# An attention kernel with an MLP woven into it: the first MLP product and its Gelus in two blocks of four, and the second product four slots later

## The chip, the cores and the metric

The kernel runs on one core of a Trainium2 chip. The metric is the device time of one execution in microseconds (us), lower being better. Five engines work side by side, each through its own list of instructions in order: TensorE (PE, with PEld for its weight loads), VectorE (DVE), ScalarE (ACT), GpSimd (POOL) and SyncE (SP), which starts most DMA transfers. They wait for each other through semaphores.

## The reference, cut to what matters

The input is eight images of 256 channels x 1024 positions in float32. Each image goes through two stages: an attention over its 1024 positions with 8 heads, and then, on the tokens, a linear attention and an MLP on a downsampled band. The parts that matter here:

```python
# stage 1, per image: softmax attention over 1024 positions, 8 heads
qkv = einsum('oc,bcl->bol', w_qkv, group_norm(x)) + b_qkv
weight = softmax(einsum('bct,bcs->bts', q * scale, k * scale))
x = x + (w_proj @ einsum('bts,bcs->bct', weight, v) + b_proj)
# stage 2, per image: linear attention, then the MLP on the low band
t = t + linear_attention(layer_norm(t))
ll, lh, hl, hh = haar(layer_norm(t))
h = gelu(einsum('bfc,hc->bfh', interp(ll), fc1_w) + fc1_b)     # 1024 hidden
ll_new = einsum('bfh,oh->bfo', h, fc2_w) + fc2_b               # back to 128
t = t + inverse_haar(ll_new, lh, hl, hh)
```

## The kernel before, in words

**Slots.** Stage 1 of an image is cut into 64 units, one for each of the 8 heads and each block of 128 keys. A unit is a 128x1024 tile of scores. TensorE makes it (`scores`, line 636), VectorE takes the row maxima (`maximum`, line 1025), ScalarE takes the exponential and its sums (`exponentials`, line 887), and every four units TensorE multiplies the result with the values (`weigh_values`, line 651, into `ps_o`), after VectorE has inverted the sums (line 1031) and GpSimd has scaled the values with them (line 1297). There are two score buffers, `ps_s0` and `ps_s1`: the scores of unit s+2 wait for the exponential of unit s. A unit's number within its image is called its slot here.

**What fills the slots.** Everything else is put into the slots by tables, one for each engine and kind of image (`PE_STEADY`, `ACT_STEADY`, `DVE_STEADY` and so on). An entry such as `"fc2": (51, 53, 55, 56)` says after which unit each piece of a step is put into that engine's list. Within a slot the pieces stand in the order of the table's keys. While image i is in stage 1, stage 2 of image i-1 and the first steps of image i+1 run in its slots. The first image has no stage 2 beside it. Images 1 to 6 use the steady tables, the last image uses `PE_LAST` and its like, which lack the steps for a next image, and stage 2 of the last image runs alone in an epilogue (`PE_TAIL` and so on). The order is fixed when the program is built: an engine whose next instruction waits does nothing else.

In TensorE's list slot s begins with the scores of unit s+1. In the lists of ScalarE and VectorE it begins with the exponential or the maximum of unit s. So an exponential "50" is the one that opens slot 50 on ScalarE.

**The work banks.** All pieces but the scores and `ps_o` share two banks, `work0` and `work1`, in turn (`banks`). A piece waits until the one before it in its bank has been read (`claim`, `READ`). The second MLP product adds four pieces into one bank (fc2 0 to 3, entries 1 to 3 in `LATER_STEPS`), so from fc2 0 to fc2 3 all other pieces go to the other bank.

**The MLP.** `ll` (line 777) makes the low band, ScalarE copies it to `band` (line 968). `fc1` n, of eight (line 782), multiplies `band` with 128 columns of the first weights, and ScalarE puts the Gelu of it into `hid` (line 971; the profile calls it `shared`). `fc2` (line 787) waits for all eight Gelus, VectorE adds the bias and subtracts the old band (line 1184), SyncE spreads the rows (line 543), and VectorE adds them to the output in slots 1 and 5 of the next image (`late_up`, line 1191). `pk0`, the first two key projections for the next image (line 663), lies among them in slots 52 and 53: ScalarE reads it as the high part (line 928), then VectorE as the low part (line 1070). `rT` are transposes (line 698) that ScalarE copies out (line 975).

Of the kernel before, what the change touches and what calls it, by code (L numbers as in the profile page):

```python
# [42 lines left out]
for _name, _width in (("bq", 2), ("bk", 2), ("bproj", 2), ("bqk", 4), ("lepe_w", 6), ("lepe_bias", 6),  # L43
# [37 lines left out]
    "values": (2, 6, 10, 14, 18, 22, 26, 30, 34, 38, 42, 46, 50, 54, 58, 62),  # L81
}
ACT_STEADY = {
    "copy": (3, 4, 34, 35), "x1T": (9, 10, 11, 14), "lnT": (15, 15, 16, 16),
    "qk": (18, 18, 21, 22, 24, 25, 28, 30), "den": (32,), "rT": (47, 50, 50, 51), "ll": (48,),
    "fc1": (49, 49, 49, 49, 49, 49, 49, 49), "pq1": (11, 13), "pk1": (20, 20), "apply": (41, 41), "pq0": (43, 44),
    "pk0": (52, 53),
}
DVE_STEADY = {
# [5 lines left out]
}  # L95
# [6 lines left out]
PE_LAST = {  # L102
    "proj": (4, 5, 7, 8), "x1T": (9, 9, 10, 13), "lnT": (15, 15, 16, 16), "qk": (17, 18, 21, 22, 24, 25, 28, 29),
    "kT": (23, 26, 30, 31), "kv": (28, 33), "den": (31,), "denT": (32,), "out": (35, 37, 41, 42),
    "uT": (39, 40, 43, 43), "rT": (48, 48, 50, 51), "ll": (48,), "fc1": (48, 48, 49, 49, 49, 49, 49, 49),
    "fc2": (53, 54, 56, 57), "pq1": (11, 12), "pv1": (0, 0), "pk1": (19, 19),
    "values": (2, 6, 10, 14, 18, 22, 26, 30, 34, 39, 43, 46, 50, 55, 58, 63),
}
ACT_LAST = {
    "copy": (3, 4, 36, 39), "den": (31,), "x1T": (9, 10, 11, 14), "lnT": (15, 15, 16, 16),  # L110
    "qk": (18, 18, 21, 22, 24, 25, 28, 30), "rT": (47, 48, 51, 53), "ll": (48,),
    "fc1": (49, 49, 49, 49, 49, 49, 49, 49), "pq1": (11, 13), "pk1": (19, 20),
}
DVE_LAST = {
# [5 lines left out]
}  # L120
POOL_LAST = {
# [1374 lines left out]
```

How the kernel before makes its waits and increments, by code:

```python
        def load_image(eng, b):  # L440
            eng.wait_ge(made["pk1"], 2 * b)
            eng.dma_start(xg[:, :, :], x_v[b]).then_inc(x_in, DMA)
# [1 line left out]
        def stack_q(eng, b, g):  # L445
            eng.wait_ge(lo_done, 8 * b + 4 * g + 2)
            for h in range(HG):
                for row, part in enumerate((hi, hi, lo, lo)):
                    eng.dma_start(q_st[g][D * row:D * row + D, h, :].bitcast(F32),
                                 part[D * h:D * h + D, :].bitcast(F32)).then_inc(q_stacked, DMA)
# [1 line left out]
        def stack_k(eng, b, g, half, done_units=None):  # L453
            hi_k, lo_k = key_parts(b, g)
            if half == 0:
                eng.wait_ge(lo_done, 8 * b + 4 * g + 4)
            elif done_units is not None:
                eng.wait_ge(scores_ready, done_units)
            else:
                eng.wait_ge(lo_done, 4)
            cols = slice(half * HALF, half * HALF + HALF)
            signal = k_stacked_b if half else k_stacked_a
            for h in range(HG):
                for row, part in enumerate((hi_k, lo_k, hi_k, lo_k)):
                    eng.dma_start(k_st[D * row:D * row + D, h, cols].bitcast(F32),
                                 part[D * h:D * h + D, cols].bitcast(F32)).then_inc(signal, DMA)
# [1 line left out]
        def stack_first_k(eng, pieces, signals):  # L471
            eng.wait_ge(lo_done, 1 + nth_split(0, ("pk0", 0)))
            for h, row in pieces:
                part = (hi_first, lo_first, hi_first, lo_first)[row]
```

## Time and profile before

| | |
|---|---|
| median of three runs | 1381.69 us (1381.51 to 1382.86) |
| profiled execution, its own time | 1382.15 us |
| its span | 1380.4 us |
| PE / DVE / ACT / POOL busy | 88% / 72% / 64% / 34% |
| mean granted TensorE clock | 0.975 |

The span runs from the first instruction to the last; the profiled execution's own time is 1.75 us longer. Busy shares are over the whole span. In the timeline a row is one instruction, or several alike (x4), with its start, its duration, and behind it in brackets how long the engine had been idle and who released it. A row of a table of stretches has the stretch (from the span's start), its length, the busy time of PE, PEld, DVE, ACT and POOL with the instructions in brackets, the granted TensorE clock as a share of full speed, the busy share of the DMA engines and their GB/s. A matmul of float32 operands shows as two records, so one `fc1` piece is x2 and one `fc2` piece is x4.

### The profile page before, as it was taken

Reading aid. Unit: us, or ns where it says so; the run is one execution under the profiler, and the core shown is the slowest. Engines: PE = TensorE matmul, PEld = TensorE weight load, DVE = VectorE, ACT = ScalarE, POOL = GpSimd, SP = SyncE. Lnnn points to the kernel's source line nnn. Section 1 sums busy time; section 2 is a strip of 40 time slices with the busy share of each in tenths; the row PEclk is TensorE's granted clock in tenths of the full one; section 3 lists DMA queues with packets and bytes.
Section 4 is the critical chain, followed back from the end, with each engine's and each line's share of the span. In section 5 each row is a group of like instructions: output and inputs, shape, how many; then the busy total and the mean of one; then the engine's idle time right before and its main releaser. Section 6 shows DMA issues by size and latency. Waiting matters only on the chain.

```text
span 1380.4 us, 21964 instructions
## 1 busy us (share of the span) xinstructions
PE 1211.1 (88%) x7868; PEld 629.9 (46%) x7868; DVE 991.3 (72%) x1607; ACT 881.9 (64%) x1457; POOL 465.6 (34%) x623
## 2 busy tenths in 40 slices
PE   6888899899988999899988999899998999878846
PEld 5544544545444454444445454444444444433433
DVE  2676688848887597857889487866889487874551
ACT  1667677576766667576776768676776767656402
POOL 2001017510384015720195014730176103830450
PEclk8999999999999999999999999999999999999977
DMA  8243324133433225233252224332341333300101
GB/s 267 54 119 73 91 63 108 48 70 97 109 76 92 54 67 132 57 75 103 67 120 71 53 81 124 60 92 71 89 112 53 69 90 84 81 31 16 46 17 46
DMA packets 51355, 111.28 MB, mean 81 GB/s; under 512 B 15504, under 2 KB 15760, under 8 KB 50992
## 3 DMA queue, kind: packets, MB, share of 16 engines
q1 hardware_dynamic: 48576, 100.85, 30.0%
q0 software_dynamic: 2480, 8.78, 2.0%
q8 instruction: 63, 1.03, 0.3%
q14 instruction: 44, 0.36, 0.1%
q10 hardware_dynamic: 192, 0.26, 0.1%
HBM read 21.75 MB, written 8.39 MB: 22 GB/s over the span
## 4 chain that ended last, share of the span: by engine, by line
PE 44%; DVE 29%; POOL 8%; ACT 8%; issue 6%; SPq 3%; DMA 2%; DVEq 0%; POOLq 0%; ACTq 0%
DVE negmax L1025 15%; PE ps_s L636 10%; PE ps_o L651 7%; ACT probs L887 6%; PE work L663 4%; PE work L710 4%; POOL x L1356 4%; PE work L724 4%; PE work L782 4%; DVE ln_st L1090 3%; DVE tok L1101 3%; PE work L787 3%; POOL csum L1353 1%; DVE t L1177 1%; DVE lo L1070 1%
## 5 line engine op out<-in xcount | busy, mean ns | idle before, releaser
L887 ACT ACTIVATE probs<-ps_s,negmax 128x1024 f32<-128x1024 f32 x512 | 569.7, 1113 | 322.2 <-DVE negmax L1025 314.9
L1025 DVE TENSOR_REDUCE negmax<-ps_s 128x1 f32<-128x1024 f32 x512 | 620.0, 1215 | 192.1 <-PE ps_s L636 189.6
L636 PE MATMUL ps_s<-q_st,k_st 128*128 128x512 f32 x1024 | 404.6, 478 | 59.4 <-ACT probs L887 49.3
L636 PEld LDWEIGHTS ps_s<-q_st,k_st 128*128 128x128 f32 x1024 | 164.8, 191 | 285.5 <-ACT probs L887 167.0
L651 PE MATMUL ps_o<-probs,v_scaled 128*32 128x512 f32 x2048 | 248.8, 603 | 2.8 <-POOL v_scaled L1297 2.8
L1297 POOL TENSOR_TENSOR v_scaled<-v_tok,rsums 128x128 f32<-128x128 f32 x128 | 51.2, 400 | 545.0 <-DVE rsums L1031 544.2
L663 PE MATMUL work<-xg,w_qkv 128*128 128x512 f32 x256 | 119.6, 592 | 0.0
L724 PE MATMUL work<-ln_ch,w_qk 128*128 128x512 f32 x236 | 113.8, 604 | 2.1 <-DVE k_ch L1203 2.1
L651 PEld LDWEIGHTS ps_o<-probs,v_scaled 128*32 128x32 f32 x2048 | 53.7, 109 | 127.0 <-issue 119.8
L1356 POOL TENSOR_TENSOR x<-x,csum 128x1024 f32<-128x1024 f32 x45 | 106.8, 2373 | 2.0
L887 ACT ACTIVATION_READ_ACCUMULATOR probs<-ps_s,negmax 128x1 f32 x512 | 99.1, 194 | 0.0
L782 PE MATMUL work<-band,w 128*128 128x512 f32 x116 | 59.2, 645 | 9.1 <-ACT band L968 6.1
L663 PEld LDWEIGHTS work<-xg,w_qkv 128*128 128x128 f32 x256 | 48.2, 189 | 40.9 <-issue 33.4
L675 PEld LDWEIGHTS work<-w_qkv,xg 128*128 128x128 f32 x512 | 63.2, 196 | 4.0 <-DVE lo L1070 1.4
L675 PE MATMUL work<-w_qkv,xg 128*128 128x128 f32 x512 | 63.6, 279 | 0.0
L724 PEld LDWEIGHTS work<-ln_ch,w_qk 128*128 128x128 f32 x236 | 42.6, 190 | 41.6 <-issue 29.3
L1328 POOL TENSOR_TENSOR ln_var<-ln_mv,con 128x2 f32<-128x2 f32 x64 | 13.6, 212 | 129.0 <-DVE ln_mv L1095 129.0
L710 PE MATMUL work<-att,w_proj 128*128 128x512 f32 x120 | 56.8, 597 | 0.0
L787 PE MATMUL work<-shared,w 128*128 128x512 f32 x112 | 53.2, 597 | 1.4 <-ACT ln_ch L975 1.4
L1353 POOL TENSOR_SCALAR csum<-ln_ch,par 128x1024 f32<-128x1024 f32 x45 | 53.8, 1195 | 0.0
L971 ACT ACTIVATE shared<-work,par 128x512 f32<-128x512 f32 x58 | 39.3, 686 | 14.9 <-PE work L782 14.8
L1331 POOL TENSOR_TENSOR ln_rs<-ln_var,con 128x2 f32<-128x2 f32 x64 | 44.7, 699 | 5.0
(150 smaller groups left out, 1418.5 us busy)
## 6 DMA issues: line engine op xcount, KB each, us to landing
q_st<-hi SPq DMA_DIRECT2D x128, 128.0 KB, 2.4
q_st<-lo SPq DMA_DIRECT2D x120, 128.0 KB, 2.4
k_st<-t SPq DMA_DIRECT2D x224, 64.0 KB, 2.0
k_st<-hi SPq DMA_DIRECT2D x128, 64.0 KB, 2.0
k_st<-lo SPq DMA_DIRECT2D x128, 64.0 KB, 2.0
x<-in_x SPq DMA_DIRECT2D x8, 1024.0 KB, 4.8
out_x<-ln_ch SPq DMA_DIRECT2D x16, 512.0 KB, 2.7
xg<-in_x POOLq DMA_DIRECT2D x7, 1024.0 KB, 5.7
```

Of the source, the lines that this page charges most:

```text
L636: mm = pe.matmul(ps_s[s % 2][:, half * HALF:half * HALF + HALF], k_st[:, h, j * P:j * P + P], q_st[g][:, h, half * HALF:half * HALF + HALF ...
L651: mm = pe.matmul(ps_o[D * h:D * h + D, cols], v_scaled[:, j % 2, D * h:D * h + D], probs[:, j % 2, h, cols], start=(j == 0), stop=(j == NB ...
L663: mm = pe.matmul(bank(tile)[:, :], w_qkv[:, c, col:col + P], xg[:, c, half * HALF:half * HALF + HALF], start=(c == 0), stop=(c == NC - 1))
L675: mm = pe.matmul(bank(tile)[:, P * n:P * n + P], xg[:, c, P * nb:P * nb + P], w_qkv[:, c, col:col + P], start=(c == 0), stop=(c == NC - 1))
L710: mm = pe.matmul(ps[:, :], w_proj[:, g, P * c:P * c + P], att[:, g, half * HALF:half * HALF + HALF], start=(g == 0), stop=(g == 1))
L724: mm = pe.matmul(ps[:, :], w_qk[:, c, col:col + P], ln_ch[:, c, 1 + half * HALF:1 + half * HALF + HALF], start=(c == 0), stop=(c == NC - 1))
L782: pe.matmul(ps[:, :], w1[:, P * n:P * n + P], band[:, :], start=True, stop=True)\
L787: mm = pe.matmul(ps[:, :], w2[:, k, :], hid[:, k, :], start=(k == 0), stop=(k == 7))
L887: act.activation(probs[:, j % 2, h, :], ps_s[s % 2][:, :], ACT.Exp, bias=negmax[:, s % 4:s % 4 + 1], accum_out=sums[:, j % 2, h:h + 1]).th ...
L1025: dve.tensor_reduce(negmax[:, s % 4:s % 4 + 1], ps_s[s % 2][:, :], AX_X, ALU.max, negate=True)\
L1353: pool.tensor_scalar(lepe_product, ln_ch[:, c, tap:tap + L], param("lepe_w", 3 * c + tap), param("lepe_bias", 3 * c + tap), ALU.mult, ALU. ...
L1356: pool.tensor_tensor(x1[:, c, :], x1[:, c, :], lepe_product, ALU.add).then_inc(lepe_step, 1)
```

## The change

Only the tables of the steady images and of the last one are changed. On TensorE, fc1 4 to 7 go from slot 49 to slots 54 and 55, and fc2 from slots 51, 53, 55, 56 (last image 53, 54, 56, 57) to slots 56 to 59. On ScalarE, Gelus 4 to 7 go from slot 49 to slot 55. On VectorE the step that reads fc2 goes from slot 57 (last image 58) to slot 60. The epilogue's tables stay.

```diff
 PE_STEADY = {
-    "fc1": (48, 48, 49, 49, 49, 49, 49, 49), "fc2": (51, 53, 55, 56), "pq1": (11, 12), "pv1": (0, 1),
+    "fc1": (48, 48, 49, 49, 54, 54, 55, 55), "fc2": (56, 57, 58, 59), "pq1": (11, 12), "pv1": (0, 1),
...
 ACT_STEADY = {
-    "fc1": (49, 49, 49, 49, 49, 49, 49, 49), "pq1": (11, 13), "pk1": (20, 20), "apply": (41, 41), "pq0": (43, 44),
+    "fc1": (49, 49, 49, 49, 55, 55, 55, 55), "pq1": (11, 13), "pk1": (20, 20), "apply": (41, 41), "pq0": (43, 44),
```

ScalarE's list in a steady image, before, from the exponential that opens slot 49 on (`probs` are exponentials, `shared` Gelus, `ln_ch` copies of `rT`, `t` high parts of `pk0`):

```order
 L887 ACTIVATE probs,sums<-ps_s,negmax 128x1024
 L971 ACT_TABLE_LOAD
 L971 ACTIVATE shared<-work,par 128x512 x8
 L887 ACT_TABLE_LOAD
 L887 ACTIVATE probs,sums<-ps_s,negmax 128x1024
 L975 COPY ln_ch<-work 128x512 x2
 L887 ACTIVATE probs,sums<-ps_s,negmax 128x1024
 L975 COPY ln_ch<-work 128x512
 L887 ACTIVATE probs,sums<-ps_s,negmax 128x1024
 L928 ACTIVATE t<-work,par 128x512
 L887 ACTIVATE probs,sums<-ps_s,negmax 128x1024
 L928 ACTIVATE t<-work,par 128x512
```

The same place now, from the exponential that opens slot 53 on:

```order
 L887 ACTIVATE probs,sums<-ps_s,negmax 128x1024
 L928 ACTIVATE t<-work,par 128x512
 L887 ACTIVATE probs,sums<-ps_s,negmax 128x1024 x2
 L971 ACT_TABLE_LOAD
 L971 ACTIVATE shared<-work,par 128x512 x4
 L887 ACT_TABLE_LOAD
 L887 ACTIVATE probs,sums<-ps_s,negmax 128x1024 x12
```

In slot 49 four Gelus are left between a pair of table loads, and four others stand with a second pair of table loads behind the exponential of slot 55.

TensorE's list in a steady image, before, from the pieces of slot 51 on (`work<-con,t` is rT 2 and 3, `work<-shared` fc2, `work<-xg` pk0, `ps_s` scores):

```order
 L698 MATMUL work0<-con,t2 128x128 x4
 L787 MATMUL work1<-shared,w2 128x512 x2
 L636 MATMUL ps_s1<-q_st1,k_st 128x512 x2
 L663 MATMUL work0<-xg,w_qkv 128x512 x2
 L636 MATMUL ps_s0<-q_st1,k_st 128x512 x2
 L787 MATMUL work1<-shared,w2 128x512 x2
 L663 MATMUL work0<-xg,w_qkv 128x512 x2
 L636 MATMUL ps_s1<-q_st1,k_st 128x512 x2
 L651 MATMUL ps_o<-probs,v_scaled 32x512 x8
 L636 MATMUL ps_s0<-q_st1,k_st 128x512 x2
 L787 MATMUL work1<-shared,w2 128x512 x2
```

TensorE's list now, from the second `pk0` piece in slot 53 on (`work<-band` is fc1):

```order
 L663 MATMUL work0<-xg,w_qkv 128x512 x2
 L636 MATMUL ps_s1<-q_st1,k_st 128x512 x2
 L782 MATMUL work1<-band,w1 128x512
 L782 MATMUL work0<-band,w1 128x512
 L651 MATMUL ps_o<-probs,v_scaled 32x512 x8
 L636 MATMUL ps_s0<-q_st1,k_st 128x512 x2
 L782 MATMUL work1<-band,w1 128x512
 L782 MATMUL work0<-band,w1 128x512
 L636 MATMUL ps_s1<-q_st1,k_st 128x512 x2
 L787 MATMUL work1<-shared,w2 128x512 x2
 L636 MATMUL ps_s0<-q_st1,k_st 128x512 x2
 L787 MATMUL work1<-shared,w2 128x512 x2
```

The two `pk0` pieces, which shared `work0` while fc2 held `work1`, now lie in different banks; fc1 4 and 5 stand in front of the values product of slot 54, and the fc2 pieces follow one another in neighbouring slots.

## Rows read from the trace of the kernel before

**Rows 1.** The page, busy time and share of each engine.

```profile
PE 1211.1 (88%) x7868; PEld 629.9 (46%) x7868; DVE 991.3 (72%) x1607; ACT 881.9 (64%) x1457; POOL 465.6 (34%) x623
```

**Rows 2.** Groups on ScalarE: table loads, busy us and mean ns of one.

```profile
L971 ACT ACT_TABLE_LOAD x8 | 10.3, 1283 | 0.1
L887 ACT ACT_TABLE_LOAD x7 | 9.0, 1283 | 0.1
```

**Rows 3.** Stretches of image 4: between exponentials 49, 50, 56 and 61.

```profile
759.75:770.86 11.11, 10.26 (x36) 4.22 (x40) 2.45 (x2) 9.18 (x14) 0.00 (x0) 1.00 0.32 70
770.86:786.35 15.49, 14.71 (x63) 6.97 (x55) 7.59 (x9) 9.82 (x18) 0.40 (x1) 1.00 0.06 13
786.35:795.59 9.24, 8.54 (x47) 4.55 (x45) 6.66 (x7) 5.94 (x10) 0.80 (x2) 1.00 0.43 104
```

**Rows 4.** Timeline of image 4 from exponential 49 to Gelu 3.

```profile
759.75 1.13 ACT L887 ACTIVATE probs<-ps_s,negmax 128x1024 f32<-128x1024 f32 x1
760.99 1.28 ACT L971 ACT_TABLE_LOAD   x1
762.28 1.26 ACT L971 ACTIVATE shared<-work,par 128x512 f32<-128x512 f32 x2
...
765.05 0.69 ACT L971 ACTIVATE shared<-work,par 128x512 f32<-128x512 f32 x1 [0.17 <-PE work L782]
```

**Rows 5.** Timeline of image 4, slots 51 to 55.

```profile
773.79 1.12 ACT L887 ACTIVATE probs<-ps_s,negmax 128x1024 f32<-128x1024 f32 x1
...
775.38 1.03 PE L636 MATMUL ps_s<-q_st,k_st 128*128 128x512 f32 x2
...
776.24 1.88 PE L663 MATMUL work<-xg,w_qkv 128*128 128x512 f32 x4
776.42 1.11 ACT L887 ACTIVATE probs<-ps_s,negmax 128x1024 f32<-128x1024 f32 x1 [0.94 <-DVE negmax L1025]
777.68 0.90 PE L636 MATMUL ps_s<-q_st,k_st 128*128 128x512 f32 x2
...
780.13 1.88 PE L663 MATMUL work<-xg,w_qkv 128*128 128x512 f32 x4
...
782.70 1.11 ACT L887 ACTIVATE probs<-ps_s,negmax 128x1024 f32<-128x1024 f32 x1
782.83 0.75 DVE L1070 SCALAR_TENSOR_TENSOR t<-work,par,t 128x512 fp32r<-128x512 f32 x1 [2.01 <-ACT t L928]
```

**Rows 6.** Timeline of image 4, slots 55 to 58.

```profile
784.26 0.73 PE L636 MATMUL ps_s<-q_st,k_st 128*128 128x512 f32 x2
...
784.81 1.11 ACT L887 ACTIVATE probs<-ps_s,negmax 128x1024 f32<-128x1024 f32 x1 [0.92 <-DVE negmax L1025]
784.83 1.88 PE L787 MATMUL work<-shared,w 128*128 128x512 f32 x4
785.03 1.22 DVE L1025 TENSOR_REDUCE negmax<-ps_s 128x1 f32<-128x1024 f32 x1 [0.32 <-PE ps_s L636]
...
787.01 1.88 PE L787 MATMUL work<-shared,w 128*128 128x512 f32 x4
...
788.33 1.02 PE L636 MATMUL ps_s<-q_st,k_st 128*128 128x512 f32 x2
...
790.45 1.92 PE L651 MATMUL ps_o<-probs,v_scaled 128*32 128x512 f32 x16
```

**Rows 7.** Timeline of SyncE in image 4, the spreading of the band.

```profile
793.88 2.51 SPq L543 DMA_DIRECT2D csum<-band  x4
```

**Rows 8.** Timeline of VectorE, `late_up` in slot 1 of the next image.

```profile
802.41 1.22 DVE L1191 SCALAR_TENSOR_TENSOR ln_ch<-csum,ln_ch 128x1024 f32<-128x1024 f32 x1
```

**Rows 9.** Stretch of image 3 between exponentials 49 and 50.

```profile
600.55:612.38 11.83, 11.58 (x36) 4.93 (x40) 2.45 (x2) 9.28 (x13) 0.00 (x0) 0.86 0.28 63
```

**Rows 10.** Stretches of the last image between exponentials 50, 56 and 61.

```profile
1248.07:1259.69 11.62, 9.56 (x47) 4.21 (x40) 6.09 (x6) 8.06 (x15) 0.40 (x1) 1.00 0.00 0
1259.69:1269.64 9.95, 8.20 (x34) 3.44 (x34) 6.86 (x8) 5.94 (x10) 0.40 (x1) 1.00 0.24 53
```

More of the change, by code:

```diff
@@ L104 @@
     "kT": (23, 26, 30, 31), "kv": (28, 33), "den": (31,), "denT": (32,), "out": (35, 37, 41, 42),
-    "uT": (39, 40, 43, 43), "rT": (48, 48, 50, 51), "ll": (48,), "fc1": (48, 48, 49, 49, 49, 49, 49, 49),
-    "fc2": (53, 54, 56, 57), "pq1": (11, 12), "pv1": (0, 0), "pk1": (19, 19),
+    "uT": (39, 40, 43, 43), "rT": (48, 48, 50, 51), "ll": (48,), "fc1": (48, 48, 49, 49, 54, 54, 55, 55),
+    "fc2": (56, 57, 58, 59), "pq1": (11, 12), "pv1": (0, 0), "pk1": (19, 19),
     "values": (2, 6, 10, 14, 18, 22, 26, 30, 34, 39, 43, 46, 50, 55, 58, 63),
@@ L111 @@
     "qk": (18, 18, 21, 22, 24, 25, 28, 30), "rT": (47, 48, 51, 53), "ll": (48,),
-    "fc1": (49, 49, 49, 49, 49, 49, 49, 49), "pq1": (11, 13), "pk1": (19, 20),
+    "fc1": (49, 49, 49, 49, 55, 55, 55, 55), "pq1": (11, 13), "pk1": (19, 20),
 }
```

4 rows, old and new, of tables (DVE_LAST, DVE_STEADY) are left out of this document.

## The prediction, written before the changed kernel ran

> **What bounds the kernel now.** I read the page first. TensorE is busy for 88% of the span and ScalarE for 64% [rows 1], so on average TensorE comes first and ScalarE has room. The change touches one stretch of each image, though, so I went to the groups on ScalarE next. There the table loads are to be seen: 8 in front of Gelus and 7 back to exponentials, 1283 ns each [rows 2]; the eighth Gelu block is the epilogue's. Each image pays the way out and back once.
>
> Then I cut image 4 into stretches at the exponentials. The slot of the Gelus takes 11.11 us, the next six slots 15.49 us and five more 9.24 us. TensorE is busy for 10.26, 14.71 and 8.54 us of these [rows 3], so over the 35.84 us it has only 2.33 us of gaps that show, and 0.70 of these lie in the last five slots. Two things bound the stretch by turns: the Gelu block, where exponentials wait behind ScalarE's list, and TensorE's own list in slots 50 to 57.
>
> At last I read the timeline. In the Gelu block ScalarE sets the pace: exponential 49 starts at 759.75, the table load at 760.99 and Gelus 0 and 1 at 762.28. Gelu 3 starts at 765.05, behind a wait, since fc1 2 and 3 can only be made once Gelus 0 and 1 have freed their banks [rows 4]. Outside the block I take four delays from the rows. From the start of an exponential to the scores that wait for it it is 1.26 us (776.42 to 777.68). From scores to the next piece on TensorE it is 0.86 us where TensorE had not been waiting (775.38 to 776.24) [rows 5], and 0.57 us where it had (784.26 to 784.83). From scores to their maximum it is 0.77 us and the maximum takes 1.22. A `pk0` or fc2 piece takes 1.88 us to its end and 1.32 us to the next piece (787.01 to 788.33) [rows 6].
>
> **The change part by part, steady image.** I write it down in image 4's times, all from exponential 50 on to be read 3.80 us earlier.
>
> Block A, slot 49. Four Gelus stay, with both loads. From exponential 49 to the start of Gelu 3 it is 5.30 us; 0.69 of Gelu, 1.28 of load and 0.04 of steps between them bring exponential 50 at 7.31 in place of 11.11 us [rows 3, 4]. Gain: 3.80 us.
>
> Slots 50 to 55. fc2 0 and 1 are gone from here, and `pk0` 1 no longer waits for the bank of `pk0` 0. Exponential 50 to 52 stay: ScalarE waits there for rT copies and for a maximum that VectorE does only after inverting sums. Scores 53 start 0.32 us earlier, at 775.06, where exponential 51 (773.79) lets them go; `pk0` 0 then starts at 775.63 and ends at 777.5, and its high part is read in front of exponential 53, at 778.2. Scores 54 wait for exponential 52 and stay at 777.68. Now `pk0` 1 follows them directly, at 778.25 in place of 780.13, ScalarE can read its high part at 780.2, and exponential 54 starts at 780.8 in place of 782.70 [rows 5]. Exponential 55 keeps its distance of 2.1 us (782.70 to 784.81 [rows 6]), since the low part (0.75) and the maximum (1.22) stand between: 782.85. Gain: 1.95 us.
>
> Block B, slot 55. It adds two loads and four Gelus behind exponential 55. fc1 4 is made before, at 780.5, and fc1 5 after the low part of `pk0` 1 has been read, at 781.65; both are ready when the load ends. TensorE does the values product and scores 56 in the meantime (to 785.4), so it loses little by fc1 6 waiting for Gelu 4. The block has block A's shape: 7.31 us to exponential 56 (790.15) where it was 1.54. Cost: 5.77 us. As exponential 56 stood at 786.35, the three parts together give -3.80 - 1.95 + 5.77 = 0.0 us there. I bound block B by 6.5 us (loads and Gelus alone: 1.24 + 2 x 1.30 + 4 x 0.66) and 8.5 us (TensorE late by 1.2 us, its extra wait for the low part), and take 7.31, the nearest row.
>
> The Trainium skill speaks against such a split: "ScalarE: Activation LUTs", in "Rules for kernel authors", says to group functions by table set and finish one set before switching. The same page, in "What ACT_TABLE_LOAD costs", puts a switch at about 2.66 us, a load of 1283 ns and a drain as long again. This trace agrees with the load only: Gelu 0 starts 1.29 us after the load does, and the load 1.24 us after exponential 49 [rows 4]. By the page 14 more switches would cost some 37 us of ScalarE's time, by the rows 18 us; my sum uses neither, but block B as timed.
>
> Slots 56 to 60. Here lie all four fc2 pieces now, of which two came before exponential 56 until now and a third just before. fc2 0 waits for Gelu 7 and runs at 788.9, under the load back to exponentials, at no cost. Exponential 57 follows exponential 56 by 1.20 us (791.35), its maximum being ready. Scores 58 wait for exponential 56: 791.41; exponential 58 comes at 793.45. fc2 1 stands at 791.98, so scores 59 come at 793.3 and exponential 59 at 795.65. fc2 2 (794.2) and the values product (795.5, 1.92 long [rows 6]) stand in front of scores 60, at 797.4: exponential 60 at 799.5. fc2 3 (798.0) makes scores 61 start at 799.3, and in front of maximum 61 VectorE now waits for fc2 3 (799.9) and does the band's step (0.75): exponential 61 at 801.95, where it was 795.59. From exponential 56 on that is 11.80 us in place of 9.24 [rows 3]. Cost: 2.56 us. Bounds: 1.2 us, if half of it is covered by the gaps, and 3.44 + 0.75 = 4.2 us, if two fc2 pieces of 1.72 and the step lie bare. After slot 61 units go at their round trip from exponential to scores to maximum to exponential, through which a delay passes whole: `pv0` 1 and slot 63 keep their distances.
>
> The move of VectorE's step delays SyncE's list as well: the spreading of the band, now at 793.88 and 2.51 us long [rows 7], starts some 7 us later (800.7). Behind it are queued the late keys, not wanted before slot 16, and waiting for it is `late_up` in slot 1, at 802.41 [rows 8], now 808.8. From the last issue to `late_up` it was 6.0 us (796.4 to 802.4) and is 5.6 us now (803.2 to 808.8). Cost: none; without this cover each microsecond of lateness would stand in every image.
>
> Per steady image: 0.0 + 2.56 = 2.56 us, six times: 15.4 us.
>
> Last image. It has no `pk0`. Block A gives 3.80. Taking fc2 0 out of slot 53 brings exponential 55 about 0.9 us earlier. The slot of block B grows from 2.75 us to 7.3, so the six slots take 11.62 - 0.9 + 4.55 = 15.3 us; the next five take 12.5 in place of 9.95 [rows 10]. That is -3.80 + 3.65 + 2.55 = 2.4 us. I take 2.3. First image and epilogue are unchanged.
>
> **Sum:** 1382.15 of the profiled execution + 15.4 + 2.3 = 1399.85 us. The median of the runs shown is 0.46 below that execution, so I predict 1399.4 us. A change under 0.2% (2.8 us) counts as none.
>
> **Rivals.** (1) Faster: fc2 hides in the gaps. TensorE stands at 88%, and behind block B two score tiles wait ready, so units could run at their round trip, which is 1.26 + 0.77 + 1.22 + 0.1 = 3.35 us for two slots: exponential 57 after 1.20 and four more at 1.68 make 7.9 us, 1.3 less than before. Seven images: 9.2 us, 1372.5. It decides whether TensorE has room for 3.44 us of fc2 where 0.70 us of gaps showed [rows 3]; for it speaks that ScalarE idles a third of the time, against it that a slot with fc2 takes 0.86 + 1.32 = 2.18 us already. (2) No change: the delay of slots 56 to 61 is caught up in slots 61 to 63, so only the 0.0 us at exponential 56 remains: about 1382. Against it: a round trip bounds those slots. (3) Slower still: the clock. TensorE now idles about 1.3 us in front of scores 53, 0.7 before scores 54 and 0.6 before scores 58. In image 3 the granted clock was 0.86 of full speed on average in the slot of the Gelus, a piece of it at 1.2 GHz, and that slot took 11.83 us in place of 11.11 [rows 3, 9]. If each of seven images pays such 0.7 us once or twice more, it is 5 to 10 us on top: about 1407.
>
> **How the numbers follow.** Forecast 0.72, its own range 1391 to 1408 (1.2 us up or down per image, by the bounds above); rival 3 0.14; rival 1 0.07; rival 2 0.05; a switch that stops ScalarE for twice its load, 0.02, at 1417, by another 1.28 for each of 14 loads (this is where the page's drain would lead; against it stands Gelu 0's start, [rows 4]). Range 1389 to 1410, which leaves out rivals 1 and 2 and the upper end of 3. Faster 0.07, the same 0.05, slower 0.88.
>
> **What would show it.** Table loads: 15 in front of Gelus and 14 back, at 1283 ns. Between exponentials 49 and 50: 7.3 us. Between 50 and 56: 19.3. Between 56 and 61: 11.8, with fc2 between scores in each slot. `pk0` 1 some 1.9 us after the scores 54 no more. I am wrong if slots 56 to 61 take under 9.3 us, if block B takes under 6 us, or if the band's landing holds `late_up`.

## The result, and the profile after

The changed kernel takes 1404.56 us (median of four runs, 1402.84 to 1407.14) against 1381.92 us before: the ratio is 1.0164, with a 95% interval of 1.0144 to 1.0184. A second set of four runs on another occasion gave 1403.17 us, a ratio of 1.0144 (1.0120 to 1.0168) to the kernel before as it ran there, 1383.14 us. Slower, then, and within the range; the forecast of +17.7 us was 5 us short of the median. The profiled execution took 1402.84 us with a span of 1401.0 us, 20.6 us more than the span of before. What follows is about these 20.6 us.

On the page TensorE's and ScalarE's shares stay almost where they were [rows 1]:

```profile
PE 1216.1 (87%) x7868; PEld 631.1 (45%) x7868; DVE 992.8 (71%) x1607; ACT 898.6 (64%) x1471; POOL 465.5 (33%) x623
```

ScalarE is busy for 16.7 us more, with 14 instructions more. The 14 are table loads, 7 in front of Gelus and 7 back, each as long as before [rows 2]:

```profile
L971 ACT ACT_TABLE_LOAD x15 | 19.2, 1283 | 0.3
L887 ACT ACT_TABLE_LOAD x14 | 18.0, 1283 | 0.2
```

The stretches of image 4 answer to [rows 3], cut at exponentials 49, 50, 55, 56 and 61 (length, busy time of PE, PEld, DVE, ACT and POOL, granted clock, DMA share, GB/s):

```profile
767.96:775.25 7.29, 6.44 (x28) 3.03 (x32) 2.45 (x2) 6.42 (x9) 0.00 (x0) 1.00 0.49 106
775.25:787.32 12.07, 9.72 (x40) 4.51 (x36) 6.18 (x7) 8.59 (x16) 0.40 (x1) 1.00 0.01 2
787.32:794.60 7.28, 6.09 (x27) 2.33 (x26) 2.53 (x3) 6.41 (x9) 0.40 (x1) 1.00 0.44 106
794.60:806.73 12.13, 11.66 (x55) 5.93 (x53) 5.64 (x6) 5.91 (x11) 0.40 (x1) 1.00 0.10 24
```

| image 4, us | before | foretold | after |
|---|---|---|---|
| exponential 49 to 50 | 11.11 | 7.31 | 7.29 |
| 50 to 55 | 13.95 | 12.00 | 12.07 |
| 55 to 56 (block B) | 1.54 | 7.31 | 7.28 |
| 56 to 61 | 9.24 | 11.80 | 12.13 |
| together | 35.84 | 38.42 | 38.77 |

Exponential 56 stands 26.64 us after exponential 49 where it stood 26.60 us after it: the first three terms cancel, as foretold, and the loss comes to light behind it. The same figures repeat within 0.02 us in all six steady images, but for slot 49 of image 6, 8.11 us long.

Block B is a copy of block A. Its timeline:

```profile
787.32 1.11 ACT L887 ACTIVATE probs<-ps_s,negmax 128x1024 f32<-128x1024 f32 x1 [0.92 <-DVE negmax L1025]
788.54 1.28 ACT L971 ACT_TABLE_LOAD   x1
789.83 1.26 ACT L971 ACTIVATE shared<-work,par 128x512 f32<-128x512 f32 x2
790.57 1.98 PE L782 MATMUL work<-band,w 128*128 128x512 f32 x4 [0.78 <-ACT shared L971]
...
792.60 0.69 ACT L971 ACTIVATE shared<-work,par 128x512 f32<-128x512 f32 x1 [0.17 <-PE work L782]
...
793.30 1.28 ACT L887 ACT_TABLE_LOAD   x1
793.43 1.95 PE L787 MATMUL work<-shared,w 128*128 128x512 f32 x4 [0.41 <-ACT shared L971]
794.60 1.11 ACT L887 ACTIVATE probs<-ps_s,negmax 128x1024 f32<-128x1024 f32 x1
```

TensorE waits for ScalarE twice in it: 0.78 us in front of fc1 6 and 0.41 us in front of fc2 0. fc2 0 does run under the second load. Slots 51 to 54, answering to [rows 5]:

```profile
779.45 0.73 PE L636 MATMUL ps_s<-q_st,k_st 128*128 128x512 f32 x2 [1.34 <-ACT probs L887]
...
782.08 0.73 PE L636 MATMUL ps_s<-q_st,k_st 128*128 128x512 f32 x2 [0.18 <-ACT probs L887]
...
782.65 1.88 PE L663 MATMUL work<-xg,w_qkv 128*128 128x512 f32 x4
...
786.15 1.12 PE L782 MATMUL work<-band,w 128*128 128x512 f32 x2 [0.30 <-DVE t L1070]
```

`pk0` 1 follows scores 54 by 0.57 us (782.08 to 782.65), where it came 2.45 us after them (777.68 to 780.13 [rows 5]). TensorE idles for 1.34 us in front of scores 53, since nothing stands there any more to fill the wait. fc1 5 waits for the low part of `pk0` 1, as foretold. Slots 57 to 61, answering to [rows 6]:

```profile
798.60 1.88 PE L787 MATMUL work<-shared,w 128*128 128x512 f32 x4
...
800.41 1.92 PE L651 MATMUL ps_o<-probs,v_scaled 128*32 128x512 f32 x16
802.26 0.73 PE L636 MATMUL ps_s<-q_st,k_st 128*128 128x512 f32 x2
802.83 1.88 PE L787 MATMUL work<-shared,w 128*128 128x512 f32 x4
803.03 1.23 DVE L1025 TENSOR_REDUCE negmax<-ps_s 128x1 f32<-128x1024 f32 x1 [3.01 <-PE ps_s L636]
...
804.75 0.75 DVE L1184 SCALAR_TENSOR_TENSOR band<-work,par,band 128x512 f32<-128x512 f32 x1 [0.41 <-PE work L787]
```

Maximum 60 waits 3.01 us for its scores, behind fc2 2 and the values product, and VectorE waits again, 0.41 us, for fc2 3. From the fc2 piece to the values product it is 1.81 us, not the 1.32 us that separates such a piece from scores.

The band still comes in time. SyncE spreads it from 805.53 on and `late_up` runs at 813.54, 5.6 us after the last issue (it was 6.0 [rows 7, 8]):

```profile
805.53 2.42 SPq L543 DMA_DIRECT2D csum<-band  x4
```

```profile
813.54 1.22 DVE L1191 SCALAR_TENSOR_TENSOR ln_ch<-csum,ln_ch 128x1024 f32<-128x1024 f32 x1
```

The last image, answering to [rows 10]. Its slot 49 took 11.10 us before:

```profile
1236.97:1248.07 11.10, 10.25 (x36) 4.22 (x40) 2.45 (x2) 9.17 (x14) 0.00 (x0) 1.00 0.01 1
```

After, cut at exponentials 49, 50, 56 and 61:

```profile
1253.71:1261.83 8.12, 7.87 (x28) 3.69 (x32) 2.45 (x2) 6.53 (x10) 0.00 (x0) 0.79 0.00 0
1261.83:1277.34 15.51, 11.88 (x47) 4.90 (x40) 6.09 (x6) 13.27 (x21) 0.40 (x1) 0.89 0.00 1
1277.34:1290.13 12.79, 11.97 (x44) 5.21 (x43) 6.96 (x9) 6.02 (x10) 0.40 (x1) 1.00 0.00 1
```

It takes 36.42 us where it took 32.67: +3.75 us. The first row is 0.8 us longer than block A elsewhere, at a granted clock of 0.79, which means part of it at 1.2 GHz. The second row holds another fall of the clock, to 0.89 on average. Before, the clock was full in all of these slots.

Added up between exponentials 49 and 61: six images at +2.93 us are 17.6, less 0.7 because the clock fell in the Gelu block of two of them before and of one after, and +3.75 for the last image: 20.6 us. The other stretches differ by up to 2 us each way (the start of the program +1.9, slots 29 to 43 of the six images -1.2 together) and cancel.

### The profile page after: what moved, and what is told of

It is laid out like the page before. It is cut to its first block, busy times and chain, and to the rows that moved or that the text cites. A ratio compares the mean times of both kernels' runs of the same rounds, so it can differ in the third digit from the quotient of the medians.

```text
span 1401.0 us, 21978 instructions
## 1 busy us (share of the span) xinstructions
PE 1216.1 (87%) x7868; PEld 631.1 (45%) x7868; DVE 992.8 (71%) x1607; ACT 898.6 (64%) x1471; POOL 465.5 (33%) x623
## 4 chain that ended last, share of the span: by engine, by line
PE 40%; DVE 30%; ACT 11%; POOL 7%; issue 7%; SPq 4%; DMA 2%; DVEq 0%; POOLq 0%; ACTq 0%
DVE negmax L1025 15%; PE ps_s L636 9%; ACT probs L887 7%; PE ps_o L651 7%; PE work L710 4%; PE work L724 4%; PE work L663 3%; DVE ln_st L1090 3%; POOL x L1356 3%; DVE tok L1101 3%; PE work L787 3%; PE work L782 3%; SPq L468 1%; DVE lo L1070 1%; DVE t L1177 1%
## 5 line engine op out<-in xcount | busy, mean ns | idle before, releaser
L782 PE MATMUL work<-band,w 128*128 128x512 f32 x116 | 62.5, 656 | 16.4 <-ACT shared L971 8.8
```

What stands on the lines that cost most here:

```text
L782: pe.matmul(ps[:, :], w1[:, P * n:P * n + P], band[:, :], start=True, stop=True)\
```

## The experiments

Two theories stood at first. Theory A was the prediction's: TensorE's list sets the pace here, the split cancels against slots 49 to 55, and the late fc2 pieces are the cost. Theory B was that the cost is the 14 table loads, 14 x 1.28 = 18 us, which happens to give the same total.

### One block of Gelus, fc2 late (e1)

```diff
-    "fc2": (51, 53, 55, 56)    # PE, steady; last image (53, 54, 56, 57)
+    "fc2": (56, 57, 58, 59)
-    "fc2": (57,)               # DVE, steady; last image (58,)
+    "fc2": (60,)
```

> The kernel before, with one block of eight Gelus in slot 49 as it was, and only fc2 moved to slots 56 to 59 (VectorE's step to slot 60). Two table loads per image as before. Theory A (the cost comes from the fc2 pieces packed into slots 56 to 59, while the split itself is paid back by slots 50 to 55): slot 49 stays at 11.1 us, exponentials 50 to 55 take 12.0 in place of 13.95 us, exponentials 55 to 61 about 14.0 in place of 10.8 us, together +1.3 us in each of seven images: 1391 us. Theory B (the cost is the 14 added table loads, 18 us in all, and the place of fc2 costs nothing): the same as before, 1382 us, or less, down to 1369 if the 1.95 us of slots 52 to 54 stay gained.

Measured: 1397.42 us, ratio 1.0107 (1.0082 to 1.0132). Image 4, exponentials 49, 50, 56, 61:

```profile
763.80:774.90 11.10, 10.25 (x36) 4.21 (x40) 2.45 (x2) 9.17 (x13) 0.00 (x0) 1.00 0.33 71
774.90:788.52 13.62, 10.49 (x51) 4.72 (x44) 7.49 (x9) 9.80 (x18) 0.40 (x1) 1.00 0.06 15
788.52:801.28 12.76, 12.76 (x59) 6.77 (x58) 6.86 (x7) 6.02 (x11) 0.80 (x2) 1.00 0.28 69
```

The gain of 1.9 us in the middle row and the loss of 3.5 us in the last are there without any added load: +1.64 us per steady image, which I had put at 1.3. The last image loses 4.8 us (37.46 for 32.67), but part of that is the clock: its slot 55 ran wholly at 1.2 GHz and took 4.93 us.

```profile
1267.52:1272.45 4.93, 4.87 (x19) 1.24 (x19) 1.23 (x1) 1.21 (x4) 0.00 (x0) 0.50 0.00 0
```

Theory B alone is out, since it allowed 1382 us at most. Theory A had the direction but not the size: it had said 1391 us. But the changed kernel has 1.29 us more per image than this one, so the split was not free.

### One block of eight in slot 55 (e2)

```diff
-    "fc1": (48, 48, 49, 49, 49, 49, 49, 49), "fc2": (51, 53, 55, 56)   # PE
+    "fc1": (54, 54, 55, 55, 55, 55, 55, 55), "fc2": (56, 57, 58, 59)
-    "fc1": (49, 49, 49, 49, 49, 49, 49, 49)                            # ACT
+    "fc1": (55, 55, 55, 55, 55, 55, 55, 55)
```

> fc2 as in the changed kernel (56 to 59), all eight fc1 pieces and Gelus in one block in slots 54 and 55, so two table loads per image. Theory A: slot 49 falls from 11.1 to about 2 us, 52 and 53 give 1.95 us, slot 55 takes 11.1 in place of 1.54 us, slots 56 to 60 cost 2.6 us as in the changed kernel: +1.1 us per image, about 1390 us. Theory B: no added loads, so 1382 us, the time of before.

Measured: 1406.77 us, ratio 1.0174 (1.0147 to 1.0200). Both theories missed, at 1390 and 1382 us. Image 5, exponentials 50, 55 and 56:

```profile
934.04:947.29 13.25, 11.44 (x53) 5.27 (x55) 7.40 (x8) 8.59 (x16) 0.40 (x1) 1.00 0.15 32
947.29:958.38 11.09, 9.91 (x35) 3.52 (x34) 2.53 (x3) 9.16 (x13) 0.40 (x1) 1.00 0.40 95
```

Slot 49 fell to 1.78 us and slot 55 grew to 11.09, as expected, but slot 50 grew from 2.94 to 4.13 us, so slots 50 to 54 gained 0.7 and not 1.95 us, and in two images they took 15 us at a lower clock. A Gelu block gives something back: while ScalarE is held, TensorE makes the next scores, a first pair of transposes and the values product of slot 50. Without the block, slot 50 has this product to do itself, and ScalarE waits 1.97 us there for the transposes behind it. The stretch from 49 to 61 takes 38.25 us, +2.4, with no load added.

### Relu for Gelu in both kernels (e3, e4)

```diff
-    act.activation(hid[:, n, :], ps[:, :], ACT.Gelu, bias=param("b1", n)).then_inc(gelu_done, 1)
+    act.activation(hid[:, n, :], ps[:, :], ACT.Relu, bias=param("b1", n)).then_inc(gelu_done, 1)
```

The kernel before:

> The kernel before with a Relu in place of each Gelu, which takes all table loads but the first out of the program (the MLP's function is thereby another). Theory A: the first load of a block was half hidden behind fc1 0 and 1, the second behind the values product: 2 us less per image, about 1367 us. Theory B: loads stand bare, 2.57 us less in each of eight images: 1361 us.

The changed kernel:

> The changed kernel with a Relu in place of each Gelu (again another function in the MLP, no table loads but the first). To be set against the kernel before with Relu. Theory A: the two differ by 2 us or so in each image (fc2 in slots 56 to 59 costs the same, and fc2 0 has no load to hide under any more), so this runs at about 1380 us, 13 us over the other. Theory B: without loads the change costs nothing: both within 3 us.

A Relu needs no table load here: only the one at the program's start is left. Measured: 1377.49 us (ratio to the kernel before 0.9942, 0.9921 to 0.9963) and 1386.32 us (1.0015, 0.9995 to 1.0036). Neither total is as foretold: 1367 or 1361 us for the first, 1380 us by theory A for the second. In the profile of each, slot 49 took 1.7 us longer in two images at a lower granted clock (0.84 and 0.75). Runs of both scatter over 10 us, so the stretch of image 4 from exponential 49 to 61 says more. The kernel before with Relu:

```profile
757.66:792.02 34.36, 33.17 (x140) 15.80 (x140) 16.69 (x18) 22.37 (x38) 1.20 (x3) 1.00 0.24 57
```

The changed kernel with Relu:

```profile
762.37:797.87 35.50, 33.03 (x141) 16.03 (x141) 16.80 (x18) 22.11 (x39) 1.20 (x3) 1.00 0.23 53
```

Without loads the change costs 1.14 us per image; with them 2.93. Theory A had said 2 us, theory B nothing: each load pair is worth something, but less than its 2.57 us. The first pair, taken out of the kernel before, gives 1.48 us.

Cut at exponentials 49, 50, 55, 56 and 61, the changed kernel with Relu shows where each pair is paid:

```profile
762.37:767.38 5.01, 4.75 (x15) 2.64 (x16) 1.34 (x2) 3.86 (x7) 0.00 (x0) 1.00 0.72 157
767.38:780.25 12.87, 11.06 (x51) 4.96 (x53) 7.29 (x8) 8.60 (x16) 0.40 (x1) 1.00 0.01 2
780.25:785.06 4.81, 4.66 (x24) 1.74 (x23) 1.42 (x3) 3.63 (x6) 0.40 (x1) 1.00 0.44 107
785.06:797.87 12.81, 12.56 (x57) 6.70 (x57) 6.75 (x7) 6.02 (x12) 0.40 (x1) 1.00 0.18 43
```

With loads the four are 7.29, 12.07, 7.28 and 12.13 us. The first pair costs 2.28 us in slot 49 and gives 0.80 back in slots 50 to 54: 1.48 us, as in the kernel before. The second costs 2.47 us in slot 55 and gives 0.68 back behind it: 1.79 us.

### One block, fc2 late, Relu (e7)

The edit is that of e1 and of e3 together.

> One block in slot 49, fc2 in slots 56 to 59, Relu in place of Gelu (another function in the MLP, no table loads but the first). Against the changed kernel with Relu (35.50 us from exponential 49 to 61) it tells what the split costs without its loads. Theory A' (the split costs nothing but its two loads): 34.36 of the kernel before with Relu + 1.63 for the late fc2 = 36.0 us, so it is even 0.5 us per image slower than the split one. Theory D (the split costs by breaking the block, loads or not): 1.3 us faster than the split one, 34.2 us.

Measured: 1388.78 us, ratio 1.0036 (1.0018 to 1.0054). Image 4, exponentials 49 to 61:

```profile
759.91:795.91 36.00, 33.16 (x141) 15.78 (x141) 16.82 (x18) 22.43 (x38) 1.20 (x3) 1.00 0.22 52
```

36.00 us, as theory A' had it. So the late fc2 costs 1.64 us with loads or without, the split by itself saves 0.50 us (36.00 to 35.50), and the second pair of loads costs 1.79 us (38.77 - 35.50, less the first pair's 1.48 us). Theory D, at 34.2 us, is out. 1.64 - 0.50 + 1.79 = 2.93 us.

### fc2 spread over slots 56, 57, 59 and 61 (e5)

```diff
-    "fc2": (56, 57, 58, 59)    # PE; DVE (60,)
+    "fc2": (56, 57, 59, 61)    # PE; DVE (62,)
```

> The changed kernel with fc2 in slots 56, 57, 59 and 61 (VectorE's step in 62) in place of 56 to 59. Theory A (what counts is TensorE's idle time, and TensorE is never idle between scores 59 and 61 of the changed kernel, so a piece moved there only changes places): no gain, exponential 49 to 63 within 0.5 us of the changed kernel's 42.1 us, the whole within 3 us of it. Theory C (the crowding of a values product and an fc2 piece in slot 58 is itself the price, 1.9 us of the 4.2 us of slot 59): 1.9 us less in each of seven images, 13 us under the changed kernel.

Measured: 1400.77 us, ratio 1.0118 (1.0088 to 1.0149), which is 2.4 us under the changed kernel on the same chip; with four runs of each, whose times overlap, this is not clear of the scatter. Image 4, exponentials 56, 61 and 63:

```profile
794.12:804.34 10.22, 9.75 (x48) 4.99 (x47) 4.98 (x5) 5.91 (x11) 0.40 (x1) 1.00 0.11 27
804.34:808.96 4.62, 4.62 (x28) 2.01 (x27) 3.20 (x4) 2.41 (x5) 0.00 (x0) 1.00 0.01 3
```

Slots 56 to 60 are 1.91 us shorter and the two behind them 1.27 us longer (3.35 before). From 49 to 63 it is 41.48 for 42.12 us: 0.64 us won, a little more than theory A allowed and a third of theory C's 1.9. A piece moved along a list in which TensorE never idles mostly changes places.

### fc2 1 out of slot 53, the bank still held (e6)

```diff
-    "fc2": (51, 53, 55, 56)    # PE, steady images; DVE (57,)
+    "fc2": (51, 55, 56, 57)    # DVE (58,)
```

> The kernel before with fc2 in the steady images in slots 51, 55, 56, 57 (VectorE's step in 58): slot 53 loses its fc2 piece, but the bank stays held from slot 51 on, so pk0 1 must still wait for the low part of pk0 0. If the held bank is what kept exponential 54 back: slot 53 falls only from 3.9 to about 3.5 us, not to the 2.6 us of the changed kernel, and the wait of pk0 1 for VectorE grows to over 1 us. If it was the fc2 piece's time on TensorE: 2.6 us as there. In time: +0.7 us in each of six images, 4 us over before, or with the second 1.3 us less than that in each.

Measured: 1387.69 us against 1383.14, ratio 1.0029 (1.0012 to 1.0046): 4.6 us for the 4 expected. TensorE in slot 53:

```profile
778.46 1.98 PE L663 MATMUL work<-xg,w_qkv 128*128 128x512 f32 x4 [1.16 <-DVE t L1070]
```

The wait for VectorE is 1.16 us, and slot 53 takes 3.60 us, not 2.62: the held bank keeps exponential 54 back once the piece is gone that had covered this wait. The stretch takes 36.55 us, +0.71 us as expected.

### The changed kernel again (e8)

> The changed kernel itself, on the same chip as the others. Exponential 49 to 61: 38.77 us in each steady image without a fall of the clock, as before. The whole: 1402 to 1408 us, 20 us or so over the kernel before; where runs differ, slots 29 to 44 and the granted clock differ, not the stretch that was changed.

Measured: 1403.17 us. The stretches of image 4 are the same within 0.02 us: 7.29, 12.06, 7.28 and 12.14 us. The clock fell in slot 49 of two steady images here, not of one. In the profiles of before, after, e1 and e8 slots 29 to 43 of one steady image took anything from 38.4 to 40.1 us, with the same list of instructions.

### Keys first, then fc2 (e9)

```diff
-    "fc2": (51, 53, 55, 56) ... "pk0": (52, 53)   # PE, steady images
+    "fc2": (53, 54, 55, 56) ... "pk0": (51, 52)
-    "pk0": (52, 53)                               # ACT
+    "pk0": (51, 53)
```

> The kernel before (one block of Gelus in slot 49), but in the steady images pk0 goes to slots 51 and 52 and fc2 to 53 to 56 on TensorE (ScalarE reads pk0 in slots 51 and 53). No bank is held while pk0 is made, and TensorE has the same work at the same places. Theory A (only TensorE's idle time counts; 0.8 us of it lie between exponentials 50 and 56): the stretch from exponential 49 to 61 falls by 0 to 0.5 us from 35.84 us in six images, the whole by 0 to 3 us. If the held bank was worth the 1.9 us that slots 52 to 54 of the changed kernel gained: 1.9 us less in each of six images, 11 us in all.

Measured: 1383.58 us against 1383.83, ratio 0.9996 (0.9985 to 1.0008): no change. (ScalarE reads the second key piece in slot 53 as the edit shows, not in 52.) The stretch from 49 to 61 takes 35.91 us, 0.07 more than before, where theory A had said 0 to 0.5 less. Image 4, exponentials 49, 50, 56, 61:

```profile
758.81:769.91 11.10, 10.25 (x36) 4.21 (x40) 2.45 (x2) 9.17 (x13) 0.00 (x0) 1.00 0.32 71
769.91:785.49 15.58, 14.80 (x63) 6.82 (x55) 7.59 (x9) 9.77 (x18) 0.40 (x1) 1.00 0.14 34
785.49:794.72 9.23, 8.54 (x47) 4.55 (x45) 6.66 (x7) 5.94 (x11) 0.80 (x2) 1.00 0.50 115
```

Exponential 55 comes 2.6 us earlier after exponential 50 than before (11.34 for 13.95 us), and slot 55 takes 4.24 in place of 1.54 us: all of it is given back at once, since scores 56 wait behind the same work of TensorE. It was tried as a version that might beat both kernels, and does not. None of the experiments points to one that would.

**The experiments side by side.** Image 4, exponentials 49 to 61. TensorE's gaps are the length less its busy time.

| kernel | length | TensorE busy | its gaps |
|---|---|---|---|
| before | 35.84 | 33.51 | 2.33 |
| keys first (e9) | 35.91 | 33.59 | 2.32 |
| bank held (e6) | 36.55 | 33.47 | 3.08 |
| fc2 late (e1) | 37.48 | 33.50 | 3.98 |
| one block in slot 55 (e2, image 5) | 38.25 | 33.93 | 4.32 |
| changed | 38.77 | 33.91 | 4.86 |
| before, Relu (e3) | 34.36 | 33.17 | 1.19 |
| fc2 late, Relu (e7) | 36.00 | 33.16 | 2.84 |
| changed, Relu (e4) | 35.50 | 33.03 | 2.47 |

The kernel of e5 is left out, since its last fc2 piece lies behind exponential 61. TensorE's work is 33.0 to 33.9 us in all of these. What differs more is how long it stands still: of the change's 2.93 us, 2.53 are gaps and 0.40 is busy time.

## Why the prediction was right, and where it was short

**Block A, slots 50 to 55, block B.** Right within 0.1 us each: -3.82 us measured for -3.80 foretold, -1.88 for -1.95 and +5.74 for +5.77. The Gelu block's own rows gave the shape of both halves, and the two waits that I had named (fc1 6 on Gelu 4, fc1 5 on the low part) are there. That the table loads cost what the block says, and no drain beside it, holds: Gelu 4 starts 1.29 us after its load. The Trainium skill, in "ScalarE: Activation LUTs", "What ACT_TABLE_LOAD costs", adds some 1.38 us of drain to each load; by an estimate from this figure, block B with its two loads would have been 2.8 us longer. This trace disagrees: block B took 7.28 us. The rule in the Trainium skill's "Rules for kernel authors", on the same page, to do all of one table set before switching is borne out: the second pair of loads costs 1.79 us per image, and the split with it 1.29 us (e1 against the changed kernel).

**Slots 56 to 60.** The mechanism was right and the term too small: 2.56 foretold, 2.89 measured. I had set 1.3 us from fc2 2 to the values product, the distance from such a piece to scores; measured it is 1.81 us. Exponentials 57 to 59 still come within 0.1 us of the times foretold after exponential 56. Exponential 60, behind this product, is 0.41 us late, and 0.33 us are left at exponential 61. Six images: 2.0 us.

**The last image.** The term was mis-sized most: 2.3 foretold, 3.75 measured. Most of what is missing is rival 3, the clock. Slot 49 took 8.12 us at a granted clock of 0.79, and 7.28 at full clock in e8. Slots 50 to 54 took 8.23 us at 0.86, and 7.89 at full clock in e5, whose lists are the same up to there:

```profile
1253.00:1260.28 7.28, 6.43 (x28) 3.03 (x32) 2.45 (x2) 6.42 (x9) 0.00 (x0) 1.00 0.00 0
```

```profile
1260.47:1268.36 7.89, 5.37 (x24) 2.44 (x16) 4.84 (x5) 6.85 (x13) 0.40 (x1) 1.00 0.00 0
```

So the two falls cost 0.8 and 0.3 us. Put together from these rows the image would cost 2.6 us at full clock: slots 50 to 54 gain 1.0 us, for 0.9 foretold, slot 55 takes 7.28, for 7.3, and slots 56 to 60 take 12.80, for 12.5, with the same 0.3 us missing as in the steady images. e1's 4.8 us for this image are no measure of late fc2 at full clock, since its slot 55 ran at 1.2 GHz.

**The clock (rival 3).** In the steady images it did not come: the clock fell in slot 49 of one of them in the changed kernel, of two in e8 and of two before, although TensorE idled more. In the last image it did come, twice in the profiled execution and once in e8 (granted clock 0.85 in slots 50 to 54). The other profiles agree. Between exponentials 49 and 61 of the last image the clock fell in all seven profiles of kernels with fc2 late (after, e1, e2, e4, e5, e7, e8) and in none of the four that leave fc2 0 in slot 53 there (before, e3, e6, e9). In front of the fall in slots 53 and 54 of the changed kernel TensorE had waited 1.51 and 0.46 us for ScalarE.

**The 5 us above the forecast.** The profiled execution took 1402.84 us where the sum had 1399.85. Of these 3.0 us, 2.0 are the term of slots 56 to 60 and 1.5 the last image's; blocks A and B and slots 50 to 54 add 0.2, and one fall of the clock less in slot 49 of the steady images takes 0.7 off. The other 2.2 us are scatter: the median of four runs is 1.7 us above the profiled one, and I had subtracted 0.5 us for the same difference before.

**Rivals 1 and 2.** Both fell by the point from which they were to be decided: TensorE had 0.70 us of gaps after exponential 56 and 3.44 us of work to take in. It has 0.47 us left there now, and slots 61 and 62 take 3.35 us as before: nothing is caught up.

**What the sum did not tell.** The zero at exponential 56 hid three effects that the experiments took apart. Exponentials that come earlier in slots 52 to 54 are not a gain: e9 has 2.6 us of that and ends with none. The 1.9 us there were lent by fc2 0 and 1 and repaid behind exponential 56: e1 gains 1.9 us there and loses 3.5 us behind. Per image it is +1.64 us for taking fc2 out of TensorE's waits, -0.50 us for two short blocks in place of a long one (measured without loads), and +1.79 us for the second pair of loads.

## What to carry to other kernels

Where one engine's list is nearly full, write down its busy time over the whole stretch and then only ask where it will stand still: work taken out of a wait leaves the wait bare and has to be paid where it is put. An instruction of another engine that comes earlier behind such a list is not a gain until the list's own last instruction comes earlier. A change of function tables costs the part of it that the full engine can't work through; count it where it lies and not at its duration. And where work is taken out of a stretch that already has waits, as in the last image here, look at the granted clock there: it may fall, which here cost 1.2 us in one image.

## What the runs showed of the hardware that was not expected

A pair of table loads lasts 2.57 us, and taking one out saved 1.48 us in the first block and 1.79 us in the second: TensorE works under part of it, with fc1 0 and 1 or the values product and fc2 0. On ScalarE a load starts 0.02 us after the instruction before it, and the next one follows 1.29 us after the load's start, in every Gelu block but the epilogue's, where it is up to 0.11 us more.

TensorE's granted clock fell to 1.2 GHz in some Gelu blocks and not in others that have the same instructions and waits: in images 3 and 5 before, in image 6 and the last after, for 0.7 to 0.8 us each time (11.83 to 11.93 us for 11.10, 8.11 us for 7.29). In the last image the falls go with the place of fc2, as told above: seven of seven profiles with late fc2, none of four without.

From a piece of fc2 to scores behind it it is 1.31 or 1.32 us at full clock where TensorE had not waited, but from a piece of fc2 to a values product 1.81 us, in all seven images of the changed kernel and of e1.

Slots 29 to 43 vary from image to image and run to run, from 38.4 to 40.7 us in the six steady images of the eleven profiles. Part of it is the clock: the 28 stretches at full clock take 38.62 us on average and at most 39.28, the 38 in which it fell (0.96 over the stretch) take 39.64 on average. At full clock the other stretches of a steady image repeat to 0.3 us or better within one kernel. In slots 29 to 43 TensorE also stands before some of its many small products with nothing in the profile that it waits for, here in the kernel before:

```profile
1046.80 1.14 PE L764 MATMUL work<-kv_c,shared 128*128 128x128 f32 x8 [2.00 <-issue]
```

What this is was not tried and stays open. Together with the clock it is likely why runs of one kernel scatter over 4 to 11 us, which no run here shows by itself. It is in both kernels alike.
